# A hybrid block kernel: another order of outputs and loads around the attention heads, projections and memsets in another order, and three of eight query tiles by pairs

## The reference

```python
x = x + time_mix(layernorm(x))          # a recurrence over the 2048 rows, 2 heads of 64
x = x + ffn(layernorm(x))               # block F in the trace
x = x + latent_attention(layernorm(x))  # causal, 16 heads, block L
x = x + ffn(layernorm(x))               # block H, same weights as F
```

```python
h = layernorm(x, ln1_g, ln1_b)
q, k, v = h @ Wq, h @ Wk, h @ Wv                      # 16 heads of 8
attn = softmax(q @ k.T / sqrt(8))                     # not causal, 2048 x 2048 for each head
x = x + (attn @ v) @ Wo
m = layernorm(x, ln2_g, ln2_b)
x = x + top2_of_8_experts(m)
```

## Time and profile before

| what | value |
|---|---|
| median of 3 runs | 3222.56 us (3218.9 to 3228.38) |
| profiled execution, its own time | 3221.15 us |
| its span | 3219.4 us |
| TensorE, VectorE, ScalarE, GpSimd busy | 85%, 63%, 58%, 13% of the span |
| heads of F | about 542 to 1299 us of the span |
| heads of H | about 2194 to 2947 us |

### The profile page before, as it was taken

How to read it: one execution, slowest core, us unless ns; L and a number is a source line. 1 busy time by engine, 2 the same in 40 slices (tenths; PEclk the granted TensorE clock), 3 DMA queues, 4 the chain that set the end, 5 groups by cost and what they waited for, 6 DMA issues and landing times. The chain is left out here.

```text
span 3219.4 us, 63170 instructions
## 1 busy us (share of the span) xinstructions
PE 2728.3 (85%) x21001; PEld 1132.2 (35%) x21001; DVE 2021.2 (63%) x4035; ACT 1852.0 (58%) x2211; POOL 407.5 (13%) x664
## 2 busy tenths in 40 slices
PE   6788838988888889799699999949888889887998
PEld 2688832222222222344334433422222222222443
DVE  5544467877777777321488777648777778774222
ACT  4222205877777778434246656637777778776343
POOL 1222231111111111000011211101111111110000
PEclk9888857999989989899889999978989989898999
DMA  1000003111111011121111111121011011110211
GB/s 42 1 0 0 0 1 113 34 32 43 31 35 43 26 39 39 46 64 52 58 47 57 48 49 57 45 87 60 29 40 39 26 43 35 30 43 24 77 59 33
DMA packets 93530, 130.80 MB, mean 41 GB/s; under 512 B 17969, under 2 KB 60939, under 8 KB 90827
## 3 DMA queue, kind: packets, MB, share of 16 engines
q1 hardware_dynamic: 87509, 119.87, 12.0%
q10 hardware_dynamic: 5744, 7.17, 0.7%
HBM read 90.28 MB, written 23.89 MB: 35 GB/s over the span
## 5 line engine op out<-in xcount | busy, mean ns | idle before, releaser
L685 ACT ACTIVATE Fprob<-Fs 128x1024 f32<-128x1024 f32 x512 | 518.0, 1028 | 158.1 <-PE Fs L537 131.3
L685 ACT ACTIVATE Hprob<-Hs 128x1024 f32<-128x1024 f32 x512 | 518.0, 1028 | 154.2 <-PE Hs L537 126.6
L762 DVE TENSOR_REDUCE Fmaxes<-Fm 128x1 f32<-128x512 f32 x744 | 471.9, 683 | 70.2 <-PE Fm L597 61.1
L762 DVE TENSOR_REDUCE Hmaxes<-Hm 128x1 f32<-128x512 f32 x744 | 472.0, 683 | 67.6 <-PE Hm L597 58.2
L762 DVE TENSOR_REDUCE Lmaxes<-Lm 128x1 f32<-128x512 f32 (+3 forms) x640 | 354.5, 603 | 92.3 <-PE Lm L521 57.7
L685 ACT ACTIVATE Lprob<-Ls 128x1024 f32<-128x1024 f32 (+7 forms) x384 | 293.4, 778 | 168.8 <-PE Ls L537 106.3
L569 PE MATMUL Fo<-Fprob,Fvh 128*32 128x256 f32 x4096 | 338.4, 410 | 0.3 <-ACT Fprob L685 0.3
L569 PE MATMUL Ho<-Hprob,Hvh 128*32 128x256 f32 x4096 | 335.1, 406 | 0.3 <-ACT Hprob L685 0.3
L597 PE MATMUL Fm<-ka,Fqa 60*128 60x512 bf16 x744 | 235.6, 402 | 96.5 <-DVE Fmaxes L762 88.2
L597 PE MATMUL Hm<-ka,Hqa 60*128 60x512 bf16 x744 | 235.4, 402 | 95.3 <-DVE Hmaxes L762 87.5
L537 PE MATMUL Fs<-Fqa,ka 60*128 60x512 bf16 x1024 | 270.0, 404 | 1.6 <-ACT Fprob L685 1.6
(11 more groups left out here) (445 smaller groups left out, 3875.5 us busy)
## 6 DMA issues: line engine op xcount, KB each, us to landing
FEwb<-FE_weights SPq DMA_DIRECT2D x8, 1024.0 KB, 5.7
HEwb<-HE_weights SPq DMA_DIRECT2D x8, 1024.0 KB
Fvh<-vstack SPq DMA_DIRECT2D x17, 256.0 KB, 2.5
Lvh<-vstack SPq DMA_DIRECT2D x17, 256.0 KB, 2.4
Hvh<-vstack SPq DMA_DIRECT2D x17, 256.0 KB, 2.4
FEw<-in_L_ffn_W SPq DMA_DIRECT2D x16, 256.0 KB, 2.9
HEw<-in_L_ffn_W SPq DMA_DIRECT2D x16, 256.0 KB
Fqa<-F_qparts SPq DMA_DIRECT2D x34, 96.0 KB
```

The costliest lines, as they stand in the source:

```text
L685: nc.scalar.activation(prob[:, :, :].rearrange("p k q -> p (k q)")[:, lo:hi], sps[entry_slot(h, "score", a, n)][:, o:o + hi - lo], ACT.Exp ...
L762: nc.vector.reduce_max(maxes[:, a, t, kb:kb + 1], src[:, 0:n], AX.X).then_inc(max_free, 1)
```

## The change

It has four parts.

1. SP does `spread(h - 1)` ahead of the load in all attentions, not only in the causal one.
2. `PAIRED_TILES` is (1, 3, 6) and no longer (2, 5), so three of eight tiles of a half go by pairs. The planner places everything anew: 38 entries and 54 items and turns for a head.
3. In the setup the non-causal order of projections is q, pairs, k. SP stores and loads q, waits for the pairs and loads them; the scalar queue stores pairs and k. k is no longer stored behind SP's loads.
4. The memsets of `ka` and `pairs` cover all 128 partitions in one piece each, and `vstack`, `topp` and `nothing` are set in `FN2`, not in `FN1`.

```diff
-PAIRED_TILES = (2, 5)
+PAIRED_TILES = (1, 3, 6)
...
-    BLOCKS = [(2, b) for b in range(NB)] + [(w, b) for w in (0, 1) for b in range(NB)] if PAIRED \
-        else [(w, b) for w in (1, 0) for b in range(NB)]
+    BLOCKS = [(w, b) for w in ((0, 2, 1) if PAIRED else (1, 0)) for b in range(NB)]
...
                     for half in range(2):
-                        if n == ends(0, half):
-                            store(act, 0, half)
-                if not PAIRED:
+                        if PAIRED and n == ends(2, half):
+                            store(act, 2, half)
+                        if PAIRED and n == ends(1, half) or not PAIRED and n == ends(0, half):
+                            store(act, 1 if PAIRED else 0, half)
+                if PAIRED:
+                    store(act, 1, 1)
+                else:
                     store(act, 0, 1)
...
                 if PAIRED:
-                    store(sp, 2, 0)
-                    store(sp, 2, 1)
+                    store(sp, 0, 0)
+                    store(sp, 0, 1)
+                    sp.wait_ge(stored[0], 32)
+                    load_q(sp, 0, 0)
                     sp.wait_ge(stored[2], 32)
                     load_pairs(sp, 0, 0)
-                    sp.wait_ge(stored[0], 32)
-                    load_q(sp, 0, 0)
-                    store(sp, 1, 0)
-                    store(sp, 1, 1)
                     sp.wait_ge(stored[1], 32)
...
                 def head(h, u, first=False, last=False):
-                    if causal and not first:
+                    if not first:
                         spread(h - 1)
                     if not last:
...
                         load(h + 2, (u + 2) % SLOTS)
-                    if not first and not causal:
-                        spread(h - 1)
                     if not first:
                         keep(h - 1)
...
-        fill = [(consts[n][:][64 * r:64 * r + 32], v) for n, v in (("ka", -1.0), ("pairs", 0.0)) for r in range(GROUPS)]
-        fill += [(consts[n][:], v) for n, v in (("vstack", 1.0), ("topp", 0.0), ("nothing", 0.0))]
+        fill = [[(consts[n][:], v) for n, v in values]
+                for values in ((("ka", -1.0), ("pairs", 0.0)), (("vstack", 1.0), ("topp", 0.0), ("nothing", 0.0)))]
...
-            normalize(nc, name + "N1", x, n1, None, consts, fill=fill)
-            normalize(nc, name + "N2", n1, n2, main, consts, col["ln1_g"], col["ln1_b"])
+            normalize(nc, name + "N1", x, n1, None, consts, fill=fill[0])
+            normalize(nc, name + "N2", n1, n2, main, consts, col["ln1_g"], col["ln1_b"], fill=fill[1])
```

More of the change, by code:

```diff
@@ L118, in attention @@
     K_LOADS = 16 * GROUPS * PARTS
+    stored = [semaphore(nc, heads, f"{name}{x}_stored") for x in ("q", "k", "pairs")]
     FIRST_ROW = [TROWS + sum(PARTS - b for b in range(a)) * DH for a in range(PARTS)]
@@ L166, in attention @@
             sem(x) for x in ("projected", "split", "high", "middle", "second", "mixed", "padded", "v_read"))
-        stored = [sem(f"{x}_stored") for x in ("q", "k", "pairs")]
         def store(engine, w, half):
@@ L1866, in build, with feed_forward @@
         consts["nothing"] = sb("nothing", [P, 8])
-        fill = [(consts[n][:][64 * r:64 * r + 32], v) for n, v in (("ka", -1.0), ("pairs", 0.0)) for r in range(GROUPS)]
-        fill += [(consts[n][:], v) for n, v in (("vstack", 1.0), ("topp", 0.0), ("nothing", 0.0))]
-        def feed_forward(name, fill=None):
-            normalize(nc, name + "N1", x, n1, None, consts, fill=fill)
-            normalize(nc, name + "N2", n1, n2, main, consts, col["ln1_g"], col["ln1_b"])
+        fill = [[(consts[n][:], v) for n, v in values]
+                for values in ((("ka", -1.0), ("pairs", 0.0)), (("vstack", 1.0), ("topp", 0.0), ("nothing", 0.0)))]
+        def feed_forward(name, fill=(None, None)):
+            normalize(nc, name + "N1", x, n1, None, consts, fill=fill[0])
+            normalize(nc, name + "N2", n1, n2, main, consts, col["ln1_g"], col["ln1_b"], fill=fill[1])
             attention(nc, name, main, G["Wq"], G["Wk"], G["Wv"], consts, yT, causal=False)
```

## The result

The changed kernel takes 3000.64 us (median of 4 runs, 2989.06 to 3007.16) against 3222.28 us before, a ratio of 0.9306 with a 95% interval of 0.9274 to 0.9339. The forecast was 2973 us with a range of 2935 to 3045. The profiled execution took 3007.16 us, the longest of the four, so it is 35 us above the 2972 us that the sum gave for it.

What follows compares the result with a forecast made beforehand. VectorE's wait for Fsums, 4.8 us a head, was taken to halt TensorE and ScalarE too. Gains of 228 (heads), 10.3 (fills) and 11 us (setup), 249 together, take 3221.15 to 2972, as median 2973 us; range 2935 to 3045.

Steps and rivals of the forecast that it cites:

- Outputs ahead of loads: In heads of F and H, earlier writes remove VectorE's 4.8 us wait for Fsums and the 3.2 us that follow it.
- The undisturbed head: In F before the change, a head without the wait takes 39.9 us, so 8.9 of 48.8 us are lost.
- Three tiles by pairs: In heads of F and H, TensorE's sum of 38.1 us stays the bound; a head takes 39.6 us before loop returns.
- my pair entry: On TensorE in a head, a pair entry with the score entry behind it and its weighing takes 1.54 us.
- small waits: TensorE's waits in a head for VectorE's buffers, 2.7 us before; the forecast head is 39.6 us against TensorE's sum of 38.1.
- Loops: In heads of F and H, TensorE's loop returns every three heads cost 0.9 us a head, and this stays.
- Fills: In layer norms FN1 and FN2, one-piece memsets and the moved ones gain 10.3 us net, once.
- Setup: Before the heads of F and H, the new order of projections, stores and loads gains 5.5 us each, 11 us together.
- entries set the pace: Rival, chance 0.18: each entry in a head still costs 1.11 us, so a head takes 43.0 us and the kernel 3043 us.
- the wait is taken over: Rival, chance 0.08: something hidden under the wait takes back 4 us a head, giving 3085 us.
- it did not matter: Rival, chance 0.02: heads stay at 48 us without the wait, only layer norms and setups gain, about 3185 us.

Runs made afterwards that it cites:

- two tiles: Changed kernel with PAIRED_TILES (2, 5) as before instead of (1, 3, 6): 3023.98 us, ratio 0.9369.
- without the reciprocal: Changed kernel with TensorE's and VectorE's head loops written out and the reciprocal of the sums left out of VectorE's division: 2909.59 us; with PAIRED_TILES (2, 5), 2929.17 us.
- late outputs: Changed kernel with spread(h - 1) behind the load again in F and H: 3192.37 us, ratio 0.9892.
- four tiles: Changed kernel with PAIRED_TILES (1, 3, 5, 7) instead of (1, 3, 6): 3007.12 us, ratio 0.9320.
- old fills: Changed kernel with all memsets in FN1 again, ka and pairs in pieces of 32 partitions: 3013.89 us, ratio 0.9339.
- outputs between: Changed kernel with spread(h - 1) behind the 14 loads of q and pairs and ahead of the 7 of k and v: 3020.89 us, ratio 0.9368.
- outputs alone: Kernel before with only spread(h - 1) moved ahead of the load: 3044.62 us, ratio 0.9434.

## Why the prediction came out as it did

**Outputs ahead of loads: right.** The wait for `Fsums` is gone, it comes back when the order is turned back, and it is a deadline with 9 us to spare, as worked out. No wait of TensorE for a load stands in the rows of the heads, so the loads that come later cost nothing that the traces show.

**The undisturbed head: the step that went wrong.** "Head 0 has no division. Its half from 565.80 to 585.74 takes 19.94 us at a clock of 1.00, so an undisturbed head takes 39.9 us." I took the half without the division twice. The division is 1.2 us of VectorE's work (0.95 and 0.29), it always falls into the other half, and TensorE stands for it behind its full buffers: the head with two tiles took 40.99 us ahead of the loops and 41.19 inside them, and 40.00 without the reciprocal. So 8.9 us lost per head were 7.6, and the base from which I judged the third tile was wrong by 1.3.

**Three tiles by pairs: direction right, size wrong twice.** I gave the third tile 0.3 us a head and TensorE's sum as the bound. It brings 0.93, since TensorE stands less for VectorE when that has four items fewer (5.0 us against 1.8 over three heads). The division is not what makes the difference: without the reciprocal the third tile still brings 0.78 (40.00 against 39.22). The head after came to 40.26 us, not 39.6. One part of that is my pair entry: I priced it by the one run of seven matmuls that begins with two items. TensorE in an undisturbed head of the changed kernel:

```profile
635.80 0.39 PE L596 MATMUL Fm<-ka,Fqa 60*128 60x512 bf16 x1
...
637.57 0.39 PE L596 MATMUL Fm<-ka,Fqa 60*128 60x512 bf16 x1
...
641.15 0.39 PE L589 MATMUL Fm<-pairs,Fqa 60*128 60x512 bf16 x2
...
642.68 0.39 PE L596 MATMUL Fm<-ka,Fqa 60*128 60x512 bf16 x1
```

The run that begins with one item takes 1.77 us, the one that begins with two takes 1.53. Three of the six runs of a head begin with one, so TensorE's own sum by these rows is 26 x 1.11 + 3 x 1.54 + 3 x 1.77 = 38.8 us and not 38.1. (The kernel before has runs of both kinds too.) The other part is the division, 0.88 of it also with three tiles; the 1.5 us that I allowed for small waits were to cover all this and did not. Over 28 heads 0.65 us are 18 us, most of the 24 us by which the heads fell short.

**Loops: mis-sized in F.** I carried 0.9 us a head over from before; it was 1.3 in F (41.59 - 40.26) and 0.85 in H (41.11 - 40.26). Against the loops written out it is 1.5 in F and 1.0 in H, as heads inside the loops are longer even where nothing returns (40.26 us in F and 40.61 in H, 40.10 written out). I put it down to TensorE's return alone, and without that return F and H cost the same.

**Fills: right,** 11.2 us against 10.3. **Setup: mis-sized,** from the traces 3.9 us in F and 3.5 in H against 5.5 each: SP's issues of the loads of q took 7.0 us instead of 4.8, with the stores of the scalar queue under way. That these stores are the cause was not tried by itself. In H the profile of the changed kernel shows less of a gain than its like: in five other runs with the new setup (two tiles, late outputs, four tiles, old fills, outputs between) the stretch in H takes 30.9 to 31.2 us, against 32.7 in it and 36.2 before.

Heads (24 us), setup (4) and the start and end of the heads (2) are 30 of the 35 us by which the profiled execution missed, less 1 for the fills. The stretch between the heads of F and the first output of L took 5 us more than before, and the heads of L 2 us more. That stretch took between 345 and 351 us in the profiles of all these kernels, and no part of the change is in it. The 5 us come in three places: 1.1 ahead of the first statistics of `FN3`, the layer norm behind the heads, 2.1 ahead of the first matmul of the experts, and 2.6 from the projections to the first items of L. With the old setup alone turned back it took 345.4 us, as before, but with the outputs alone, also with the old setup, 348.5; its cause stays open.

**The rivals.** That entries set the pace is refuted by four tiles (0.35 us for two entries, where 2.2 would follow); that the wait is taken over did not happen; that it did not matter is refuted by the late outputs. In `FN2` VectorE's short instruction took 2.92 us (0.17 with the old fills) and ended with the memset. The trace agrees here with the Trainium skill ("SBUF — State Buffer", "Who interferes with whom"), which says that whichever of VectorE in a two-port mode and GpSimd issues first keeps the shared ports for its whole instruction while the other stands.

## What to carry to other kernels

An engine that runs its list in order turns a late small transfer into a stop of all engines behind it: put the writes that someone waits for ahead of the loads that nobody waits for yet, and check by how much they make their deadline. Read the undisturbed pace from a stretch that holds every kind of work of the period, not from its best half. A loop that returns on an engine near the bound can cost several us each time; which engine's return it is shows when they are written out one by one.

## What the runs showed of the hardware

- A return of the head loop left VectorE 4.6 to 4.9 us in F and 2.3 to 2.4 in H, and TensorE 2.1 to 2.4 us in F and H and 3.5 to 3.8 in L, without an instruction. Behind most of them TensorE's granted clock was 0.50 (1.2 GHz) for some us, in F from 770 to 776; behind the first one in H it stayed at 1.00. Written out, the same code ran 16 heads with no such wait, 56 us less in all.
- The length of a memset on GpSimd did not depend on the partitions: 6144 bf16 took 5.2 us on 32 and on 128.
- Seven matmuls of 60x512 in two row groups, with the weighing behind them, took 1.53 us where two items stood first and 1.77 where one did. Why was not tried.
